# Attention pooling on one Trainium2 core: scores in the even chunk and weighted sums in the odd chunk, as two stretches

## What is computed

```python
W_b, W_c = (fc1_w[:E], fc1_w[E:])
h = relu(einsum('bse,eh->bsh', behavior_emb, W_b) + (candidate_emb @ W_c)[:, None, :] + fc1_b)
scores = einsum('bsh,h->bs', h, fc2_w[:, 0]) + fc2_b[0]
attn = softmax(scores, axis=-1)
user_interest = einsum('bse,bs->be', behavior_emb, attn)
x = concatenate([user_interest, candidate_emb], axis=1)
z = relu(x @ mlp1_w + mlp1_b)
logit = (z @ mlp2_w + mlp2_b)[:, 0]
```

## Time and profile before

| | |
|---|---|
| time, median of 3 runs | 267.22 us (266.94 to 267.6) |
| the profiled execution | 266.79 us |
| its span, from the first to the last instruction | 265.0 us |
| PE busy | 255.0 us (96% of the span) |
| DVE busy | 202.4 us (76%) |
| ACT busy | 197.0 us (74%) |
| moved by DMA | 105.73 MB |

### The profile page before, as it was taken

One profiled execution on the slowest core, in us unless ns is written; L12 is line 12 of the kernel. 1 busy time (PEld: TensorE's weight loads), 2 busy tenths in 40 slices (PEclk: granted clock), 3 DMA queues, 4 the chain that ended last, 5 costly groups with the idle time before them and its releaser, 6 DMA issues.

```text
span 265.0 us, 10864 instructions
## 1 busy us (share of the span) xinstructions
PE 255.0 (96%) x4184; PEld 214.1 (81%) x4184; DVE 202.4 (76%) x322; ACT 197.0 (74%) x478; POOL 31.1 (12%) x39
## 2 busy tenths in 40 slices
PE   8999889979999999999999999999999999999794
PEld 7556678868888888888988888888888888888663
DVE  0445977958798897979798997979798897969211
ACT  2558785967969696988978797979696895958220
POOL 2000202002020201102020201102020300303010
PEclk9999999999999999999999999999999999999999
DMA  7999999999999999999999999999999999999800
GB/s 244 433 425 422 431 417 427 423 426 422 422 433 425 425 429 421 433 425 425 429 421 433 427 423 429 421 433 425 425 429 421 433 425 425 429 420 425 369 10 0
DMA packets 10684, 105.73 MB, mean 399 GB/s; under 512 B 1328, under 2 KB 1712, under 8 KB 2864
## 3 DMA queue, kind: packets, MB, share of 16 engines
q1 hardware_dynamic: 10384, 105.37, 94.5%
q10 hardware_dynamic: 288, 0.20, 0.2%
HBM read 105.56 MB, written 0.00 MB: 398 GB/s over the span
## 4 chain that ended last, share of the span: by engine, by line
PE 94%; issue 2%; DVE 2%; ACT 1%; POOL 0%; DVEq 0%; ACTq 0%; POOLq 0%
PE z_ps L661 17%; PE s_ps L675 17%; PE z_ps L665 16%; PE z_ps L662 16%; PE u_ps L687 16%; PE z_ps L656 5%; PE z_ps L790 2%; PE z_ps L687 1%; PE z_ps L726 1%; PE s_ps L746 1%; PE z_ps L761 1%; PE z_ps L767 1%; ACT hidden_first L414 1%; DVE xl L508 0%; PE z_ps L774 0%
## 5 line engine op out<-in xcount | busy, mean ns | idle before, releaser
L508 DVE TENSOR_TENSOR xl<-xt,xh 128x800 fp32r<-128x800 f32 x116 | 113.7, 1011 | 0.1
L368 ACT CAST xh<-xt 128x800 fp32r<-128x800 f32 x116 | 94.9, 879 | 16.5 <-DMA xt<-in_behavior_t 16.5
L414 ACT ACTIVATE hidden_rest<-z_ps,bias 128x200 f32<-128x200 f32 x192 | 66.5, 430 | 24.1 <-PE z_ps L665 19.3
L661 PE MATMUL z_ps<-xh,w_hi 128*128 128x512 f32 x232 | 82.4, 355 | 1.3 <-DVE hidden_rest L518 1.2
L662 PE MATMUL z_ps<-xh,w_lo 128*128 128x512 f32 x232 | 76.5, 345 | 0.0
L665 PE MATMUL z_ps<-xl,w_hi 128*128 128x512 f32 x232 | 61.9, 348 | 0.0
L661 PEld LDWEIGHTS z_ps<-xh,w_hi 128*128 128x128 f32 x232 | 43.5, 188 | 15.6 <-issue 3.8
L339 POOL TENSOR_TENSOR weights_by_row<-weights,masks_sb 128x400 f32<-128x400 f32 x31 | 29.1, 942 | 221.0 <-DVE xl L508 149.0
L518 DVE TENSOR_TENSOR hidden_rest<-z_ps,neg_bias 128x800 f32<-128x800 f32 x48 | 47.3, 986 | 6.2 <-PE z_ps L656 3.7
L687 PE MATMUL u_ps<-x,weights_by_row 128*32 128x128 f32 (+1 forms) x1680 | 46.4, 262 | 2.8 <-issue 2.8
L662 PEld LDWEIGHTS z_ps<-xh,w_lo 128*128 128x128 f32 x232 | 43.8, 189 | 5.2
(11 more groups left out here) (66 smaller groups left out, 105.2 us busy)
## 6 DMA issues: line engine op xcount, KB each, us to landing
x<-in_behavior SPq DMA_DIRECT2D x31, 1600.0 KB, 21.7
xt<-in_behavior_t SPq DMA_DIRECT2D x30, 1600.0 KB, 20.0
xt<-in_behavior_t SPq DMA_DIRECT2D x4, 400.0 KB, 5.0
xt<-in_behavior_t SPq DMA_DIRECT2D x2, 800.0 KB, 7.7
x<-in_behavior SPq DMA_DIRECT2D x1, 832.0 KB, 13.3
x<-in_behavior SPq DMA_DIRECT2D x1, 768.0 KB, 14.8
later_sb<-in_later SPq DMA_DIRECT2D x1, 258.5 KB, 23.9
first_sb<-in_cand_rest SPq DMA_DIRECT2D x1, 192.0 KB, 5.9
```

The source lines that it names most:

```text
L368: nc.scalar.copy(xh_of(q, g)[:, :], xt[q][:, g, :]).then_inc(xh_made, 1)
L414: op = nc.scalar.activation(hidden_of(q, g)[:, :, mine], z[:, :, mine], ACT.Relu, bias=bias[:, bass.ds(c * ROWS + g * EACH + b, 1)])
L508: nc.vector.tensor_tensor(xl[g][:, :], xt[q][:, g, :], xh_of(q, g)[:, :].bitcast(F32), ALU.subtract).then_inc(xl_made, 1)
L661: nc.tensor.matmul(z[:, a:b], w_hi[:, :], xh_of(q, g)[:, a:b], start=True, stop=False)
```

## The change

The pair's narrow matmuls are cut into two stretches. PE makes the scores of a pair in the even chunk, and the sums of another pair (the one before) in the odd chunk behind it, with `transpose_sums` ahead of them. So the sums of a pair stand one chunk later than before. Before the scores PE waits for one thing more, the copy of the last sums out of `u_ps` (`pooled4_copied`).

What hangs on the sums moves with them: on DVE `inverses` goes to the odd chunk, between `next_low(0)` and the read-out of group 2; on ACT `copy_pooled4` and `copy_pooled_t` go to the odd chunk. `weight_sums` gets a second pair of columns. On ACT the exponents of the even chunk now stand between the second and the third cast. Chunk 2 has an order of its own on ACT and DVE. At the end the candidates' part of the MLP goes ahead of the weighted sums. On SP the order in the loop is now `xt` of an even chunk c and of c + 1, then `x` of c - 4 and c - 3.

```diff
--- before.py
+++ after.py
@@ -94,7 +94,7 @@
         exp_bias = [sb(f"exp_bias{i}", [P, 1]) for i in range(2)]
         weights = [sb(f"weights{i}", [P, TILES]) for i in range(2)]
         weights_by_row = [sb(f"weights_by_row{i}", [P, TILES, 2 * ROWS]) for i in range(2)]
-        weight_sums = sb("weight_sums", [P, 2])
+        weight_sums = sb("weight_sums", [P, 2, 2])
 
         pooled4 = sb("pooled4", [P, P])
 
@@ -289,21 +289,18 @@
 
             for c in range(2, X_BUFS):
                 load_transposed(c, None)
-            load_transposed(X_BUFS, 0)
-            load(0, None)
-            load(1, None)
-            for c in (X_BUFS + 1, X_BUFS + 2):
+            for c in (X_BUFS, X_BUFS + 2):
                 load_transposed(c, c - X_BUFS)
-            load(2, None)
-            load(3, None)
+                load_transposed(c + 1, c + 1 - X_BUFS)
+                load(c - X_BUFS, None)
+                load(c + 1 - X_BUFS, None)
             with sp.Fori(0, CHUNKS // X_BUFS - 2) as turn:
                 for j in (0, 2):
-                    c = turn * X_BUFS + (2 * X_BUFS - 1 + j)
-                    load_transposed(c, (X_BUFS - 1 + j) % X_BUFS)
-                    load_transposed(c + 1, j)
-                    load(c - 3, j)
-                    load(c - 2, j + 1)
-            load_transposed(LAST, LAST % X_BUFS)
+                    c = turn * X_BUFS + (2 * X_BUFS + j)
+                    load_transposed(c, j)
+                    load_transposed(c + 1, j + 1)
+                    load(c - X_BUFS, j)
+                    load(c + 1 - X_BUFS, j + 1)
             sp.dma_start(later_sb[:, :], later).then_inc(later_loaded, 16)
             for c in range(CHUNKS - X_BUFS, LAST):
                 load(c, c % X_BUFS)
@@ -367,16 +364,17 @@
 
                 nc.scalar.copy(xh_of(q, g)[:, :], xt[q][:, g, :]).then_inc(xh_made, 1)
 
-            def exponents(c, buf, steps, early):
+            def exponents(c, pair, buf, steps, early):
                 act.wait_ge(softmax_step, steps)
                 if not early:
 
                     act.wait_ge(masked, c - 1)
 
-                    act.wait_ge(row_sums_done, c - buf)
+                    if not isinstance(c, int) or c >= X_BUFS:
+                        act.wait_ge(row_sums_done, c - buf - 2)
                 nc.scalar.activation(weights[buf][:, :].rearrange("p (r t) -> p r t", t=RUN), score_runs(buf), ACT.Exp,
                                      bias=exp_bias[buf][:, :],
-                                     accum_out=weight_sums[:, buf:buf + 1]).then_inc(weights_made, 1)
+                                     accum_out=weight_sums[:, pair, buf:buf + 1]).then_inc(weights_made, 1)
 
             def copy_pooled4(c, bank):
 
@@ -401,8 +399,8 @@
             def biased_relu(c, q, g, phase):
 
                 act.wait_ge(z_done, c * GROUPS + (g + 1))
-                if g == 1 and phase == FIRST and q % 2 == 0:
-                    copy_pooled_t(c - X_BUFS - 1, beside_z(q, g))
+                if g == 1 and phase in (FIRST, LAST) and q % 2 == 1:
+                    copy_pooled_t(c - X_BUFS - 2, beside_z(q, g))
                 if g == 1 and phase in (0, 2):
                     act.wait_ge(bias_made, phase // 2 + 1)
                 if phase >= (X_BUFS if q % 2 == 0 and g == 1 else 2) and (q % 2 == 0 or g == 1):
@@ -437,6 +435,7 @@
                     return
                 if phase == LAST:
                     biased_relu(c, q, 1, phase)
+                    copy_pooled4(c - X_BUFS, u_ps)
                     biased_relu(c, q, 3, phase)
                     return
                 if phase == 1:
@@ -447,25 +446,31 @@
                     next_half(0)
                     biased_relu(c, q, 1, phase)
                     next_half(1)
+                    if phase == FIRST:
+                        copy_pooled4(c - X_BUFS, u_ps)
                     biased_relu(c, q, 3, phase)
                     next_half(2)
                     return
                 if phase >= WHOLE:
                     high_half(c, q, 3, None, False)
+                if phase == 2:
+                    next_half(0)
                 biased_relu(c, q, 1, phase)
-                for g in range(GROUPS):
-                    next_half(g)
+                if phase > 2:
+                    next_half(0)
+                next_half(1)
 
                 for n in range(2):
-                    exponents(c - 2 + n, n, pair_steps(c - 2) + 2 * (PAIR_STEPS - 1 + n), phase == 2)
-                if phase > 2:
-                    copy_pooled4(c - X_BUFS + 1, u_ps)
+                    exponents(c - 2 + n, (q + 2) % X_BUFS // 2, n, pair_steps(c - 2) + 2 * (PAIR_STEPS - 1 + n), phase == 2)
+                next_half(2)
+                next_half(3)
                 biased_relu(c, q, 3, phase)
 
             periods(period, (CHUNKS - FIRST) // X_BUFS - 1)(act)
             copy_pooled_t(LAST - 4, last_pair_ps[:, P:P + 2 * ROWS])
             for n in range(2):
-                exponents(LAST - 1 + n, n, pair_steps(LAST - 1) + 2 * (PAIR_STEPS - 1 + n), False)
+                exponents(LAST - 1 + n, (LAST - 1) % X_BUFS // 2, n, pair_steps(LAST - 1) + 2 * (PAIR_STEPS - 1 + n),
+                          False)
             copy_pooled4(LAST - 2, u_ps)
             copy_pooled_t(LAST - 2, u_ps[:, P:P + 2 * ROWS])
             relu(0)
@@ -577,6 +582,7 @@
                 biased_max(c, q, 0, phase)
                 if phase == LAST:
                     low_half(c, q, 3)
+                    inverses(c - X_BUFS - 1)
                     biased_max(c, q, 2, phase)
                     return
                 if phase == 1:
@@ -594,10 +602,14 @@
                 if phase == 2:
                     shifts()
                     dve.wait_ge(shift_step, 3)
+                    next_low(0)
                 for n in range(PAIR_STEPS):
                     softmax(c - 2, n, phase == 2)
-                if phase > 2:
-                    inverses(c - X_BUFS)
+                if phase == 2:
+                    biased_max(c, q, 2, phase)
+                    next_low(1)
+                    next_low(2)
+                    return
                 next_low(0)
                 next_low(1)
                 biased_max(c, q, 2, phase)
@@ -736,7 +748,7 @@
                         start=True, stop=True, tile_position=(0, g * Q))
                 op.then_inc(shift_done, 1)
 
-            def row_sums(c, scores_of):
+            def row_sums(c, pair, scores_of):
 
                 pe.wait_ge(weights_made, c + 2)
 
@@ -744,7 +756,7 @@
                 for n in range(2):
                     for g in range(GROUPS):
                         op = nc.tensor.matmul(row_sums_ps[g * Q:(g + 1) * Q, :], pair_rows[n],
-                                              weight_sums[:, n:n + 1], start=n == 0, stop=n == 1,
+                                              weight_sums[:, pair, n:n + 1], start=n == 0, stop=n == 1,
                                               tile_position=(0, g * Q))
                 op.then_inc(row_sums_done, 2)
 
@@ -804,21 +816,22 @@
                     if phase == 3 and g == 3:
 
                         pe.wait_ge(shift_step, 1)
+
                     if g == PHASE_AT and phase >= 2 and q % 2 == 0:
                         if phase == 2:
                             shift_sums()
                             pe.wait_ge(f2_col_made, 2)
                         else:
-                            transpose_sums(c - X_BUFS - 1, beside_z(q, g))
-
 
                             pe.wait_ge(softmax_step, pair_steps(c - 4) + 2)
+                            pe.wait_ge(pooled4_copied, c - 2)
                         score(c - 2, (q - 2) % X_BUFS)
                         score(c - 1, (q - 1) % X_BUFS)
-                        if phase > 2:
-                            weighted_sum(c - 4, q)
-                            row_sums(c - 4, c - 2)
-                            weighted_sum(c - 3, (q + 1) % X_BUFS)
+                    if g == PHASE_AT and phase == FIRST and q % 2 == 1:
+                        transpose_sums(c - X_BUFS - 2, beside_z(q, g))
+                        weighted_sum(c - 5, (q - 1) % X_BUFS)
+                        row_sums(c - 5, (q - 1) // 2, c - 3)
+                        weighted_sum(c - 4, q)
 
             periods(period, (CHUNKS - FIRST) // X_BUFS)(pe)
             pe.wait_ge(later_loaded, 16)
@@ -828,16 +841,16 @@
             pe.wait_ge(softmax_step, pair_steps(LAST - 3) + 2)
             score(LAST - 1, (LAST - 1) % X_BUFS)
             score(LAST, LAST % X_BUFS)
+            for m in range(2):
+                mlp_candidates(0, m)
             weighted_sum(LAST - 3, (LAST - 3) % X_BUFS)
-            row_sums(LAST - 3, LAST - 1)
+            row_sums(LAST - 3, (LAST - 3) % X_BUFS // 2, LAST - 1)
             weighted_sum(LAST - 2, (LAST - 2) % X_BUFS)
             for m in range(2):
-                mlp_candidates(0, m)
-            for m in range(2):
                 mlp_pooled(0, m)
 
```

(8 more changed lines are left out.)

## The result

The changed kernel takes 304.77 us (median of 4 runs, 304.4 to 305.2), the kernel before 267.08 us beside it: a ratio of 1.141, 95% interval 1.139 to 1.143. The forecast was 295.7 us with a range of 290.0 to 300.5. The kernel became slower, as forecast, and through the wait that was forecast; the time lies 4.3 us above the range.

What follows compares the result with a forecast made beforehand. PE (96% busy) and DMA (15.3 us per pair) were near their limits. Chunk 4's scores at 33.9 + 13 x 17.34, then 15.16 + 19.06, gave a span of 293.5; + 1.79 + 0.43 made 295.7 us, range 290 to 300.5.

Steps and rivals of the forecast that it cites:

- the wait that was forecast: PE, ahead of the odd chunk's group 1, waits 2.3 us per pair for DVE's read-out of group 2.
- The ring: Loop: scores, DVE's softmax, two `xl`, read-out, odd chunk's group 1, sums, four groups, scores again; 17.34 us per pair for 14.82.
- The clock: Rival, chance 0.02: idle PE falls to half clock, the group behind each wait takes twice as long, 17 us more, 313.
- The softmax: DVE's piece behind the scores in each pair, taken as 2.85 us; 0.3 us either way gave 291.5 to 299.9.
- The start: Chunk 2's new order gains 0.6 us and the moved transpose 0.24, so chunk 4's scores start at 33.9 us.
- From chunk 30 to the end: 15.16 us from chunk 30's scores to the narrow stretch behind chunk 31, then 19.06 us for the rest.
- Gaps on "issue": PE's first passes of narrow code: all three go, 2.8 us in the loop and 1.36 at the end.
- 4.3 us behind the start: Claim that all three gaps on "issue" come some 4.3 us after a narrow stretch starts, where code first runs.
- Loads: New order on SP: ACT's waits for `xt` go, nothing replaces them; DMA needs 15.3 of 17.34 us, share about 0.88.
- The cut by itself: An extra change on PE from narrow matmuls to products: free inside the wait, otherwise 0.1 to 0.25 us per pair.
- the gaps: Rival, chance 0.12: two gaps on "issue" in the first turn and one at the end remain, +4.1 us, 299.8.

Runs made afterwards that it cites:

- After: The changed kernel itself, with the narrow matmuls cut into two stretches, against the kernel before: 304.77 us, ratio 1.141.
- the version without waits: The changed kernel with chunk 2's order of DVE and ACT in all even chunks and the sums ahead of group 1 of the odd chunk: 267.40 us.

## Why the prediction was right and wrong

- **The ring: right, its number partly by luck.** Forecast 17.34 us per pair; measured 17.38 in the shorter pairs and 17.65 in the longer ones. Three runs show that this ring is the cause: DVE's order changed, the sums one group earlier, and both. With both, 304.8 becomes 267.4, while the scores and the sums stay in different chunks. The 17.38 is closer than its pieces. From the start of the scores to the first `xl` the forecast had 2.74 + 2.85 = 5.59 us, measured 5.44; from there to group 1 it had 2.84, measured 2.92; and for the rest 8.91, measured 9.02. The errors nearly cancel.
- **The clock: wrong.** This is the step that failed. The sum has no term for the clock; the forecast gave its fall 0.02, on one row: a window with one idle time of 1.45 us at a clock of 1.00. That row shows a single gap between dense stretches. After has 1.6 to 2.0 us of idle time in two pieces, 14 times (2.25 the first time), and four times the clock fell. The price was wrong as well: not one group at half speed in all 14 pairs (17 us), but four stretches of 3.4 us, 1.6 us each, 6.3 in all. The Trainium skill ("TensorE: Matmul & The Clock Gate", Part 1) says that the clock is granted by PE's activity and has two levels; this trace agrees, at 1.00 and 0.50, and I should have held it against the idle time that I had worked out myself, instead of setting it aside.
- **The softmax: one size for two.** I took 2.85 us for it, of one pair. From the start of the scores to the first `xl` it is 5.71 us in every other pair and 5.44 in the rest, and the 5.59 of the forecast lie between. Against the shorter pairs the longer ones add 0.27 us each, 1.6 us over six of the 13. In all, 234.15 us were measured between the scores of chunks 4 and 30, and 225.4 forecast; 6.3 are the clock, 1.6 the longer pairs, the other 0.8 is spread over small differences, 0.3 of them in the first pair.
- **The start: 0.9 late.** The scores in chunk 4 stood at 34.76 instead of 33.9; 0.66 of it was there in chunk 2 already (20.87 against 20.21). The near relatives of the kernel before vary here as well (20.01 to 20.76 in their traces). The step itself, 13.89 us from chunk 2 to chunk 4, was forecast at 13.7.
- **From chunk 30 to the end: right.** 15.31 us to the last scores (forecast 15.16 + 0.24), 19.1 us for the rest (19.06). So the span is 303.1 where 293.5 was forecast, 9.6 more; the median time is only 9.1 above the forecast, since it lies 0.4 below the profiled execution and not above it.
- **Gaps on "issue": right.** None is left in narrow matmuls. The reason isn't shown, and the "4.3 us behind the start" holds for two of the three: the one in chunk 6 began 56.67 - 1.45 - 51.14 = 4.08 us behind its scores.
- **Loads: right.** ACT's waits for `xt` in the loop went, nothing came in their place, and the DMA share in the loop is 0.91 at 375 GB/s where 0.88 was forecast.
- **The cut by itself: too cheap.** I had 0.1 to 0.25 us per pair; the version without waits shows 0.46, with one place more than after has. In after most of it lay under the wait (the 9.02 for 8.91 above holds the rest). It made the expectations for two of the experiments too low.
- **The range: too narrow.** With the ring alone the time would have been 298.4, inside it. The upper end had room for one thing only, the gaps. A rival that the forecast itself had named was left outside it on the strength of one row.

## What to carry to other kernels

A stretch of work on the critical engine can be the cover of a chain on another one. Before moving it, add up what the other engine must do between its release and the next thing that is wanted, and compare it with what is left in front of that. When a change puts a regular wait into TensorE's loop, look for a loss of clock on top of the wait. Here four of the six rounds with waits of 0.7 us or more and 1.25 us brought it, and the waits of at most 0.8 us in the versions with DVE's order changed or the sums moved (1.03 once) didn't. Filling the wait with matmuls that nobody needs is a quick test and was faster here than waiting. When two engines are near their limits (PE 14.8, DMA 15.3 us per pair), what is gained on one comes back as a wait on the other.

## What was not expected of the hardware

- The clock fell to one half four times in 303 us, for 3.4 us each, though no single idle time in the loop was longer than 1.25 us. With that one cut to 0.8 us the falls were gone in three of four runs (the fourth had a mean clock of 0.986 and was 3.3 us slower). Why four of the six longer rounds had a fall and two had none is open.
- A gap on "issue" can show up in broad matmuls too: 0.98 us with 8 more matmul records per odd chunk, and none with 4. The sizes of the first-turn gaps of the kernel before vary, from 1.3 to 1.9 us, between its near relatives.
- Why the softmax takes 0.27 us longer in every other pair is open. The rows of the two pairs differ at three places: the first transpose starts 0.10 us later behind the scores, the second 0.12 us later behind `part_max`, and the rest up to the first `xl` takes 0.05 us longer. The kernel before alternates too, by 0.14 us: 5.57 and 5.71 us from the scores to the first `xl`, with the reciprocal in both.
